# A transformer block on eight cores: attention steps scheduled by single matmuls, also inside products; first feed-forward products by weight pieces

## The reference, cut to what matters

```python
def ffn(x):                       # E = 8, K = 2; every token keeps both of its experts here
    g = softmax(x @ W_gate)       # 7 columns
    w = top_k(g, 2) / top_k(g, 2).sum()
    return x @ W_shared.T + (w[0] + w[1]) * (x @ W_expert.T) + bias   # same W_expert for all
def attn(x):
    q, k, v = (x @ Wq.T + bq), (x @ Wk.T + bk), (x @ Wv.T + bv)      # 16 heads of 64
    a = softmax(where(causal, q @ k.T / 8, -inf))
    return (a @ v) @ Wp.T + bp
x = x + 0.5 * ffn(layernorm(x))
x = x + attn(layernorm(x))
x = x + 0.5 * ffn(layernorm(x))
```

## Time and profile before

| | us |
|---|---|
| runs of the kernel before | 1286.38, 1287.34, 1433.44 (median 1287.34) |
| the profiled execution | 1291.16 |
| its span on the slowest core | 1289.5 |
| spans of the eight cores | 1275.2 to 1289.5 |
| TensorE busy on the slowest | 1163.5 |
| VectorE, ScalarE, POOL busy | 755.4, 741.3, 437.7 |

### The profile page before, as it was taken

How to read it: one execution, slowest core, us unless ns; L and a number is a source line. 1 busy time by engine, 2 the same in 40 slices (tenths; PEclk the granted TensorE clock), 3 DMA queues, 4 the chain that set the end, 5 groups by cost and what they waited for, 6 DMA issues and landing times.

```text
span 1289.5 us, 28541 instructions; the slowest of 8 cores (1275.2 to 1289.5 us)
## 1 busy us (share of the span) xinstructions
PE 1163.5 (90%) x9038; PEld 436.5 (34%) x9038; DVE 755.4 (59%) x1366; ACT 741.3 (57%) x936; POOL 437.7 (34%) x310
## 2 busy tenths in 40 slices
PE   3789878899999999999999999998999999898987
PEld 1334333333333333333333333332333333333343
DVE  6774797557557555445645654545756555555575
ACT  4362243377577666667666676665666666665501
POOL 3422443136035113403511523621443260515152
PEclk9899999899999999999999999999999999999999
DMA  9979645697376437424634745645574754647052
GB/s 274 314 243 272 160 114 150 171 207 203 86 187 191 103 117 215 107 90 150 190 88 126 174 127 143 198 119 155 116 221 109 235 140 151 173 142 199 14 176 82
DMA packets 209350, 207.44 MB, mean 161 GB/s; under 512 B 127283, under 2 KB 172339, under 8 KB 209206
## 3 DMA queue, kind: packets, MB, share of 16 engines
q1 hardware_dynamic: 202304, 202.42, 57.0%
q10 hardware_dynamic: 6902, 3.20, 1.0%
HBM read 117.49 MB, written 67.11 MB: 143 GB/s over the span
## 4 chain that ended last, share of the span: by engine, by line
PE 65%; DVE 11%; ACT 8%; issue 7%; DMA 4%; SPq 4%; DVEq 0%; POOL 0%; ACTq 0%; POOLq 0%
PE PS L995 14%; PE PS L982 12%; PE PS L922 10%; PE PS L899 9%; PE PS L1005 8%; PE PS L1037 6%; ACT PT L1273 4%; PE PS L930 4%; ACT ATT L1273 3%; DVE PT L1161 2%; SPq L787 2%; DVE BNS L1054 2%; DMA WQKV<-od 2%; DMA WQKV<-wte 1%; DVE DSB L1170 1%
## 5 line engine op out<-in xcount | busy, mean ns | idle before, releaser
L1273 ACT ACTIVATE PT<-PS,MB 128x1024 bf16<-128x1024 f32 (+3 forms) x428 | 400.8, 989 | 224.0 <-PE PS L899 221.8
L982 PE MATMUL PS<-WF,XT 128*128 128x512 bf16 x1024 | 247.8, 392 | 10.0 <-DVE WF L660 8.5
L995 PE MATMUL PS<-XT,WQKV 128*128 128x512 bf16 x1024 | 247.0, 389 | 8.3 <-ACT XT L1207 3.1
L1273 ACT ACTIVATE ATT<-PS,MB 128x1024 bf16<-128x1024 f32 x212 | 193.8, 965 | 81.5 <-PE PS L899 80.7
L750 POOL TENSOR_TENSOR SQ<-QKS 128x512 bf16<-128x512 bf16 x128 | 140.8, 1102 | 277.4 <-DVE QKS L1125 227.0
L899 PE MATMUL PS<-ATT 64*128 64x512 bf16 (+3 forms) x1280 | 187.8, 351 | 39.6 <-ACT PT L1273 26.5
L757 POOL TENSOR_TENSOR OTT<-OS,RR 128x512 bf16<-128x512 f32 x64 | 83.2, 1301 | 411.1 <-ACT RR L1284 411.0
L982 PEld LDWEIGHTS PS<-WF,XT 128*128 128x128 bf16 x1024 | 95.1, 100 | 149.3 <-issue 56.5
L995 PEld LDWEIGHTS PS<-XT,WQKV 128*128 128x128 bf16 x1024 | 93.3, 99 | 146.8 <-issue 54.7
L732 POOL TENSOR_TENSOR XC<-XC,BF 128x1024 f32<-128x1024 f32 x48 | 104.4, 2176 | 95.2 <-DVE XN L1083 95.2
L1110 DVE SCALAR_TENSOR_TENSOR XC<-PS,GG,XC 128x512 f32<-128x512 f32 x96 | 71.7, 749 | 100.1 <-PE PS L982 98.2
(11 more groups left out here) (104 smaller groups left out, 1067.5 us busy)
## 6 DMA issues: line engine op xcount, KB each, us to landing
XC<-x SPq DMA_DIRECT2D x30, 512.0 KB, 7.5
x1d<-XC SPq DMA_DIRECT2D x30, 512.0 KB, 4.6
XC<-x1d SPq DMA_DIRECT2D x18, 512.0 KB, 6.6
out<-XC SPq DMA_DIRECT2D x18, 512.0 KB, 4.7
ATT<-qd SPq DMA_DIRECT2D x64, 128.0 KB, 3.4
od<-OTT SPq DMA_DIRECT2D x64, 128.0 KB, 2.4
ATT<-kd SPq DMA_DIRECT2D x16, 512.0 KB, 5.1
ATT<-vd SPq DMA_DIRECT2D x16, 512.0 KB, 5.9
```

Source lines behind the costliest of these rows:

```text
L982: m = e.matmul(sbank(en), x[:, dc, t * 128:(t + 1) * 128], WF[:, dc, h * 512:(h + 1) * 512], start=(dc == 0), stop=(dc == DCN - 1))
L995: m = e.matmul(sbank(en), WQKV[:, int(w), dc, hp * 128:(hp + 1) * 128], XT2[:, i % 2, dc, :], start=(dc == 0), stop=(dc == DCN - 1))
L1273: e.activation(ptile(k)[:, 2 * m:2 * m + 2, off:512], PS[:, S_BANK + 2 * m:S_BANK + 2 * m + 2, off:512], AF.Exp, bias=MB[:, u // HPN, hp % ...
```

## The change

1. `make_order()` keeps a clock of TensorE's time instead of an account. Each step sets `need`, the time until the next may come: ScalarE's work of the step (`scalar_work`) times `slow`, the ratio of TensorE's to ScalarE's work up to the chunk deadline that leaves most time. At each of the eight matmuls of a product it is asked whether a step may come; if so inside a product, at matmul 2 to 6, an entry `pt` runs the product up to there, and the rest comes behind the step.
2. A spread `bc` comes only at the start of a product, at least 2400 ns after its unit's end, and with it the next step, if that is free. `bc` waits for a semaphore of its own, `v_ds`; VectorE copies DSB first, then OS. `os` comes two products behind `bc`.
3. One function `product` runs all five kinds, in parts. The first products of layer 0 run by pieces: matmuls 0 to 3 of tiles 0 to 3 behind sum 1, 4 and 5 behind sum 2, the rest behind sum 3, and the like for the second half. Each matmul pair of the first tile waits for its own sum. The four matmuls for the second and third bias row, the gate of chunk 1 and products of tiles 4 to 7 move ahead of sum 6 in the list.
4. The host lays the feed-forward weights out by piece, so that a load reads 4 KB in a row for each partition, and not twice 2 KB.

```diff
     ws(1)
     o.append(("ga", 0, 0))
+    o += [("pt", ("f", 0, n, 0), 4) for n in range(4)]
     ws(2)
+    o += [("pt", ("f", 0, n, 0), 6) for n in range(4)]
     o.append(("gb", 0, 0))
     ws(3)
-    o += [("br", 1), ("br", 2)] + [("bb", r, h) for r in (1, 2) for h in range(2)]
+    o += [("br", 1), ("br", 2)]
...
     o += [("s1", n, 0) for n in range(4)] + [("ga", 0, 1)]
+    o += [("bb", r, h) for r in (1, 2) for h in range(2)]
+    o += [("gb", 0, 1)] + [("f", 0, n, 0) for n in range(4, 8)]
+    o += [("pt", ("f", 0, n, 1), 4) for n in range(4)]
     ws(6)
-    o += [("gb", 0, 1), ("f", 0, 4, 0), ("f", 0, 5, 0)]
+    o += [("pt", ("f", 0, n, 1), 6) for n in range(4)]
     ws(7)
-    o += [("f", 0, 6, 0), ("f", 0, 7, 0)]
...
+def step_cols(k):
+    c, j = QUADS[k][1], QUADS[k][3]
+    return [512 - k_off(c, j + m) for m in range(2)]
+def scalar_work(k):
+    w = sum(250 + 1.68 * n for n in step_cols(k)) if k < NQUAD else 0
+    return w + 1230 * is_end(k - LAG - 1)
+def tensor_work(k):
+    n = sum(step_cols(k)) if k < NQUAD else 0
+    return 360 + 1.04 * n
+MATMUL = 213
+NDC = 8
...
+        elapsed = tensor_work(k) + min(max(0, elapsed - need), 500)
+        need = 2500
+        if k < NQUAD:
+            slow = 0
+            for i in range(QUADS[k][4] // HPN, NCHUNK):
+                until = ready[i + 1] if i + 1 < NCHUNK else total
+                todo = range(k, START[HPN * (i + 1)])
+                ahead = max(1, until - p) * NDC * MATMUL + sum(tensor_work(q) for q in todo)
+                slow = max(slow, ahead / sum(scalar_work(q) for q in todo))
+            need = scalar_work(k) * slow
+        k += 1
+        loads()
...
-            todo = NQUAD - state["k"]
-            rate = todo / max(1, total - p + 1)
-            state["acc"] = min(state["acc"] + rate, 2.0)
-            if NQUAD <= state["k"] < NQUAD + LAG:
-                late += step()
-            while state["acc"] >= 1 and state["k"] < state["avail"] and (
-                    hold <= 0 or state["k"] < state["before"]):
-                state["acc"] -= 1
-                late += step()
+            for m in range(NDC):
+                free = NQUAD <= k < NQUAD + LAG or k < avail and (hold < 0 or k < before)
+                if ends:
+                    if not m and elapsed >= 2400 and (not free or elapsed + 4 * MATMUL >= need):
+                        spread()
+                        if free:
+                            step()
+                elif free and elapsed >= need and m not in (1, NDC - 1):
+                    if m:
+                        out.append(("pt", e, m))
+                    step()
+                elapsed += MATMUL
+        out.append(e)
+        for s in stores:
+            s[1] -= 1
...
+                for dc in range(begin, upto):
+                    if kind == "f":
+                        if en[1] == 0 and n == 0 and dc % 2 == 0:
+                            summed(e, 4 * h + dc // 2)
...
-                    e.tensor_copy(OS[:, u % 2, :], PS[:, O_BANK, :])
-                    e.tensor_copy(DSB[:, u % 2, :], PS[:, D_BANK, :]).then_inc(v_oe, 1)
+                    e.tensor_copy(DSB[:, u % 2, :], PS[:, D_BANK, :]).then_inc(v_ds, 1)
+                    e.tensor_copy(OS[:, u % 2, :], PS[:, O_BANK, :]).then_inc(v_oe, 1)
```

More of the change, by code:

```diff
@@ L288, in make_order @@
     out = []
-    state = {"k": 0, "avail": 0, "acc": 0.0, "al": 0, "before": 0}
+    k = avail = before = loaded = 0
+    stored = set()
     def loads():
[L293 to L309, removed]
+        nonlocal loaded
+        while loaded < NUNIT and START[loaded + 1] <= avail and START[PRED[loaded] + 1] <= max(0, k - LAG):
+            out.append(("al", loaded))
+            loaded += 1
     heavy = [e[0] in HEAVY for e in other]
@@ L318, in make_order, with step, spread @@
     total = sum(heavy[first + 1:end + 1])
+    ready = [sum(heavy[first + 1:other.index(("v", 4 * i + 3, 1)) + 1]) + 6 for i in range(NCHUNK)]
+    elapsed = need = 0
+    ends, stores = [], []
     p = hold = wait = pend = 0
[L320 to L325, removed]
+    def step():
+        nonlocal k, elapsed, need
+        out.append(("qd", k))
+        v = k - LAG
+        if is_end(v):
+            out.append(("oe", QUADS[v][4]))
+            ends.append(QUADS[v][4])
+        if is_diag(k - 1):
+            out.append(("mk", k - 1))
+        elapsed = tensor_work(k) + min(max(0, elapsed - need), 500)
[10 more added lines that the diff above has]
+        loads()
+    def spread():
+        u = ends.pop(0)
+        out.append(("bc", u))
+        stores.append([u, 2])
     for n, e in enumerate(other):
         if e[0] == "ol":
[L329 to L340, removed]
+            while HPN * e[1] + HPN - 1 not in stored:
+                if ends:
+                    spread()
+                elif stores:
+                    u = stores.pop(0)[0]
+                    out.append(("os", u))
+                    stored.add(u)
+                else:
+                    step()
+        if e[0] == "pt" or not heavy[n]:
+            out.append(e)
+            continue
+        if n > first:
             p += 1
@@ L380 @@
         _banks = (6, 7, 0, 1, 2, 3, 4, 5)
[L381 removed]
+    if _e[0] in ("bb", "t", "ga", "f", "q", "k", "v", "n", "b2", "bc", "p") and not by_dma(_e) and _e not in SHARED:
         _b = _banks[_turn % len(_banks)]
@@ L934, in values, with product @@
                 i.then_inc(p_pv, 1)
+            done = {}
+            def product(en, upto):
+                kind = en[0]
+                begin = done.get(en, 0)
+                done[en] = upto
+                if not begin:
+                    bank_free(en)
+                if kind in ("q", "k"):
+                    i, hp = en[1], en[2]
+                    w = int(kind == "k")
+                    if not begin and hp == 0:
+                        for t in range(4):
+                            transposed(e, ("t", 1, 4 * i + t))
+                        if i == 0:
+                            e.wait_ge(a_wc, 16 if w else 8)
+                else:
+                    n, h = en[-2], en[-1]
+                    i, t = divmod(n, 4)
+                if kind == "v" and n == 0 and h == 0 and not begin:
+                    e.wait_ge(a_wc, 24)
+                if kind == "p" and not begin:
+                    if t == 0 and h == 0:
+                        e.wait_ge(d_ol[i % 2], 16 * (i // 2 + 1))
+                    if n == 0 and h == 0:
+                        e.wait_ge(a_wc, 32)
+                for dc in range(begin, upto):
+                    if kind == "f":
+                        if en[1] == 0 and n == 0 and dc % 2 == 0:
+                            summed(e, 4 * h + dc // 2)
+                        a = xt(2 * en[1], i)[:, dc, t * 128:(t + 1) * 128]
+                        b = WF[:, dc, h * 512:(h + 1) * 512]
+                    elif kind == "v":
+                        a = XT2[:, i % 2, dc, t * 128:(t + 1) * 128]
+                        b = WQKV[:, 2, dc, h * 512:(h + 1) * 512]
+                    elif kind == "p":
+                        a = otc(i)[:, dc, t * 128:(t + 1) * 128]
+                        b = WP[:, dc, h * 512:(h + 1) * 512]
+                    else:
+                        a = WQKV[:, w, dc, hp * 128:(hp + 1) * 128]
+                        b = XT2[:, i % 2, dc, :]
+                    m = e.matmul(sbank(en), a, b, start=(dc == 0), stop=(dc == DCN - 1))
+                if upto == DCN:
+                    was_filled(m, en)
             for en in ORDER:
@@ L943, in tensor_program @@
                         values(k - LAG)
+                elif kind == "pt":
+                    product(en[1], en[2])
+                elif kind in HEAVY:
+                    product(en, DCN)
                 elif kind == "t" and en not in TDMA:
```

80 lines of the change are left out of this document (26 added, 54 removed).

## The result

| | us | ratio to the kernel before, 95% interval |
|---|---|---|
| kernel before, median of 7 runs | 1287.31 | |
| changed kernel, median of 7 runs | 1272.32 | 0.9899 [0.9872, 0.9925] |
| its profiled execution, span on the slowest core (3) | 1269.8 | span before: 1289.5 |
| spans of its eight cores | 1261.6 to 1269.8 | |

The forecast's 2% bound was not reached. 1272.3 lies outside the forecast's own range (1226 to 1258) and just inside the wide one (1216 to 1276).

What follows compares the result with a forecast made beforehand. The prediction took TensorE, busy 90% of the span, to bound the kernel. Its terms summed to -47 us from the profiled 1291.2, less 3.9 for the median: 1240 us, own range 1226 to 1258, wide range 1216 to 1276.

Steps and rivals of the forecast that it cites:

- 2% bound: What a measurement of this kernel was said to tell, 1261.6 and 1313.1 us; faster by over 2% had chance 0.73.
- (a): Scores waiting for ScalarE's exponentials: steps placed by time leave 6 of 38.0 us, -32 us.
- (b): Values waiting for masked tiles: masks keep number and order, half of 11.3 us goes, -6 us.
- (c): Row-sum spreads waiting for DSB: copied first, spread at a product boundary, 1 of 9.0 us left, -8 us.
- (f): Products waiting for VectorE to read one of two banks: one unit in ten, +6 us, upper bound +25.
- (d): TensorE's granted clock after 300 us: five of seven slow stretches go with their gaps, -8 us.
- (g): First feed-forward products by weight pieces: gap before 57 us filled, tiles 4 to 7 begin slowly, -2 us.
- (e): TensorE's changes from product to step and back: 30 more at 0.11 us, +3 us; interrupted products cost nothing more.
- The slower rival: Interrupted accumulations cost more than whole ones; gain gone beyond 0.18 us each, up to 1349 us; chance 0.05.
- the wait moves to the banks: Rival: products wait for VectorE to free banks, at the upper bound, some slow clock stretches kept, 1264 us; chance 0.22.
- (h): Feed-forward weight loads laid out as 4 KB rows in place of two times 2 KB: 0 us.
- The third rival: Schedule doesn't spread as it says: deadlines and loads bunch steps or ScalarE's other work hits them, 1273 us; chance 0.13.

Runs made afterwards that it cites:

- aux_after: Changed kernel with small jobs held back until the next product's edge steps and spreads are written; ratio to the kernel before 0.9729.
- before_small_first: Kernel before, same steps, but each put down behind the small jobs that follow a product; ratio to the kernel before 1.0222.
- copies_only: Kernel before with DSB copied ahead of OS and the spread waiting for DSB's semaphore alone; ratio to the kernel before 0.9942.
- aux_old_copies: Changed kernel with edge steps ahead of small jobs, but OS copied first and spreads waiting for both copies; ratio to the kernel before 0.9793.
- start_only: Kernel before with only the change's first stage (feed-forward products by weight pieces) and layout; ratio to the kernel before 1.0003.

## Why the prediction was wrong

The direction was right and the mechanism of (a) too; the sum missed by 34 us (-13 against -47). 22 of these are one overlooked move; with it undone the change reaches -35. Of the other 12, 10 are sizes of the schedule's terms (27 us measured where 37 were forecast) and 2 the first stage. The waits below are lengths of rows in a view, and do not add up to these times.

**The step that failed** is that of (b), "the number and order of the masks stay", and of (c), "at a product boundary", and with them (f): all three took for granted that VectorE's and TensorE's other work stays where it was beside a step. It didn't. Every step and spread at an edge went behind the small jobs of its gap: the mask (and, in the old schedule, DSB) behind VectorE's normalisations, the spread behind the norms' sums. Shown by aux_after (-22 us) and by before_small_first (+29 us). The sum had no term for it.

(a) *Scores' wait*, forecast -32: measured 38.0 to 4.2, so -34 us of waits. Pairs 30 to 0. Right as to the wait; its share of the time was not measured by itself.

(b) *Masks*, -6: measured +9 us of waits; with the placement undone 11.3 and 12.0, so nothing. Spacing the steps did not help the masks: the pairs are gone, but 50 of the 256 now take over 600 ns, where 37 did.

(c) *DSB first*, -8: copies_only -7.5, aux_old_copies against aux_after 8. Right as a price of the copies; the distance of 2.4 us took nothing off this wait (8.7 us in aux_old_copies). But the spreads as a whole wait longer (17.2 for 12.6), since 15.4 us for banks came in.

(d) *Clock*, -8: -4.6 after 300 us, +4.5 ahead of 150 and +0.6 between, so nothing on core 3. In the part that the forecast was about, behind 300 us, it was sound, and the placement took most of it: with that undone the loss there is 1.6 us (median of the eight cores; 11.7 before, 8.3 in the changed kernel). Between 150 and 300 us, where I expected no change, it is 8.1 in place of 5.1. Ahead of 150 us TensorE now waits for ScalarE's normalisations before each of the four transposes of tiles 4 to 7 (one is shown), and the 80 matmuls behind them take 20.13 us, where 80 x 0.215 are 17.2. I had foreseen this in (g) and not counted it in (d). How much it costs is open: the loss ahead of 150 us (median of the eight cores) is 9.4 to 11.9 us in the profiles with the new first stage, and 6.0 to 10.0 in those with the old one. Changed kernel, TensorE, against the earlier trace rows:

```profile
23.36 8.34 PE L1039 MATMUL PS<-WF,XT 128*128 128x512 bf16 x32
33.09 0.61 PE L1062 MATMUL PS<-IDE,XN 128*128 128x128 bf16 x8 [1.39 <-ACT XN L1277]
...
44.39 20.13 PE L1039 MATMUL PS<-WF,XT 128*128 128x512 bf16 x80
...
76.98 3.42 PE L1039 MATMUL PS<-XT,WQKV 128*128 128x512 bf16 x8 [2.88 <-ACT XT L1272]
```

(e) *More changes from product to step*, +3: 202 steps stand inside products (I had estimated 260 from five of seven places; five of the six at which the edit lets a step in would give it), and busy time fell by 2.6 us, in aux_after by 9.3, to 1154.2, the clock's gain included. The change itself costs what an edge costs: from the start of three matmuls to the next step are 0.75 us (601.17 to 601.92), of six 1.41 (603.16 to 604.57), of eight 1.83 (618.97 to 620.80), so 0.10 to 0.12 us each beyond 0.215 per matmul. With 30 more of them the +3 was sound. The slower rival, which needed 0.18 us more at each interrupted product, did not occur. The Trainium skill ("TensorEngine Tiling (Array Packing)", Tiling Modes, Key Properties) says that a change of tiling mode drains TensorE; whatever a drain costs is inside these numbers.

(f) *Two banks*, +6: waits for the readers of a bank rose by 22 us (11.3 to 33.6), and with the placement undone are still 31.9. So this is the schedule's own, near the +25 that I gave as the upper bound. I had taken one unit in ten without a row that said so. The rival "the wait moves to the banks" (1264) was right in this. It is not spread over the units as I had it: with the placement undone, 3.5 us of these waits are ahead of 150 us, 19.2 between 150 and 300 (before 9.3) and 9.3 behind (before 2.0), so in the long even part they grew by 7. How the missing 10 us divide between the banks, the masks and the clock between 150 and 300 us is argued, not shown: no run changed the number of banks.

(g) *First stage*, -2: 0. TensorE's 7.12 us for the sum are gone, the first product of Q starts at 76.98 (forecast 75 to 79, before 78.57), and start_only measures 1.0003. The 1.6 us of lead do not reach the end; what takes them is open.

(h) *Layout*, 0: within start_only's 0, with (g).

The third rival (the schedule doesn't spread as it says) gave 1273, next to the measured 1272.3, for a reason that is refuted: it spreads as it says.

## What to carry to other kernels

When a planner is rewritten, compare the two orders it writes on **every** engine's queue, not only where the moved step stands beside the work that it was aligned to: which entries stand between it and the product before. Here a side effect of a loop's structure cost 22 us, more than the whole change brought (13). In a gap, put down first what the bound engine waits for next (the steps, their copies and masks), then the jobs that nobody is waiting for. And do not price a wait in a view at its length, nor at any fixed part of it: the waits for DSB, taken away by the order of two copies, gave nearly all (7.5 us for 8.4), the masks' waits of 20.5 and 11.3 us gave 10 and 6, with a stand-in that kept VectorE busier.

## What the runs showed of the hardware

An accumulation of eight matmuls can be left after its second to sixth for another tiling and another bank and be taken up later at the price of an edge, some 0.1 us (202 steps inside products; at 601 to 621 us, 0.82 us for three and 1.47 for six are the pace of the whole ones, 1.90 for eight, once the 0.17 us drawn beyond the last of each is taken off).

A mask (VectorE, 128 x 256 bf16, both inputs in SBUF) took 266 ns at the least, 284 in the median and 2215 at the most. All 50 that took over 600 ns had POOL at work beside them, of the 201 up to 300 ns 39 had (changed kernel, core 3). The Trainium skill ("SBUF — State Buffer", Who interferes with whom) says that a DVE instruction with two SBUF inputs contends with a GpSimd instruction that reads SBUF; the rows near 408 us agree (3.25 us for two masks beside 1.49 and 2.16 us of POOL). No run here took POOL's work away, so that this is the cause of the slow masks stays open.
